# Eight more sorted values before the Newton passes of a sparsemax threshold (audio tower, one core)

## The reference

```
def sparsemax(z):
    n = z.shape[-1]
    z_sorted = jnp.flip(jnp.sort(z, axis=-1), axis=-1)
    cssv = jnp.cumsum(z_sorted, axis=-1)
    r = jnp.arange(1, n + 1, dtype=z.dtype)
    support = 1.0 + r * z_sorted > cssv
    k = jnp.sum(support, axis=-1, keepdims=True)
    tau = (jnp.take_along_axis(cssv, k - 1, axis=-1) - 1.0) / k.astype(z.dtype)
    return jnp.maximum(z - tau, 0.0)
...
sim = jnp.einsum('bhid,bhjd->bhij', q, k) * SCALE
attn = sparsemax(sim)
out = jnp.einsum('bhij,bhjd->bhid', attn, v)
```

## Time and profile before

| | |
|---|---|
| median of 3 runs | 937.27 us (936.76 to 937.72) |
| the profiled execution | 943.18 us, of which the span of its instructions 941.4 us |
| PE busy | 682.3 us (72% of the span) |
| DVE busy | 614.2 us (65%) |
| ACT busy | 456.1 us (48%) |
| POOL busy | 214.3 us (23%) |
| mean granted PE clock | 0.848 |

### The profile page before, as it was taken

The page is one execution under the profiler, slowest core; times in us unless marked ns, Lnnn a source line. Parts: engine busy times, 40 slices in busy tenths (PEclk is TensorE's granted clock), DMA queues, the critical chain, the costliest instruction groups (busy, mean ns, idle before and its releaser), DMA issues.

```text
span 941.4 us, 12887 instructions
## 1 busy us (share of the span) xinstructions
PE 682.3 (72%) x3940; PEld 449.2 (48%) x3940; DVE 614.2 (65%) x2230; ACT 456.1 (48%) x663; POOL 214.3 (23%) x216
## 2 busy tenths in 40 slices
PE   5566959768996988399999998762221897667880
PEld 3234445345564564166575665441110565445660
DVE  2897568777977867697979879855668553423110
ACT  3773648437765756277778677752000331221310
POOL 1111100001000001001010010001003668888876
PEclk9878979978997998799999998885555897788895
DMA  5200000000000000000000000005000133443433
GB/s 153 77 0 1 0 2 1 2 2 13 1 2 12 1 2 12 1 2 13 1 2 13 2 13 2 13 1 151 0 0 20 43 52 67 68 68 65 68 34 28
DMA packets 34858, 23.72 MB, mean 25 GB/s; under 512 B 8246, under 2 KB 31366, under 8 KB 34768
## 3 DMA queue, kind: packets, MB, share of 16 engines
q0 software_dynamic: 11264, 8.40, 6.6%
q1 hardware_dynamic: 23292, 14.28, 5.4%
q10 hardware_dynamic: 212, 0.08, 0.0%
HBM read 14.36 MB, written 8.39 MB: 24 GB/s over the span
## 4 chain that ended last, share of the span: by engine, by line
DVE 30%; PE 29%; issue 12%; ACT 7%; POOL 7%; another core or an unknown queue 5%; DVEq 5%; DMA 2%; ACTq 1%; POOLq 0%; SPq 0%
DVE back L1043 7%; DVE top L1046 5%; PE ps L930 5%; DVE top L1036 4%; POOL out_dram L513 4%; PE ps L740 3%; PE ps L758 3%; PE ps L916 3%; PE ps L785 3%; PE ps L834 2%; PE ps L808 2%; PE ps L818 2%; ACT back L543 2%; DVE front L1236 2%
## 5 line engine op out<-in xcount | busy, mean ns | idle before, releaser
L543 ACT ACTIVATE front<-ps 128x1024 f32<-128x1024 f32 x128 | 127.8, 1026 | 41.0 <-PE ps L785 18.6
L635 ACT ACTIVATE front<-front,minus_tau 128x256 f32<-128x256 f32 x256 | 108.8, 499 | 66.1 <-DVE minus_tau L1125 65.0
L543 ACT ACTIVATE back<-ps 128x1024 f32<-128x1024 f32 x72 | 73.8, 1025 | 90.8 <-issue 74.0
L818 PE MATMUL ps<-ident,front 128*128 128x128 f32 x512 | 77.1, 300 | 52.0 <-ACTq L637 24.2
L513 POOL DMA_INDIRECT out_dram<-back x64 | 103.0, 1609 | 29.7 <-issue 18.3
L449 POOL CROSS_LANE_REDUCE more_all<-more 128x3 int32<-128x3 f32 x32 | 14.7, 460 | 410.7 <-DVEq L1062 410.7
L1043 DVE MATCH_REPLACE8 back<-top,front 128x256 f32<-128x256 f32 x256 | 101.4, 415 | 0.0
L818 PEld LDWEIGHTS ps<-ident,front 128*128 128x128 f32 x512 | 65.3, 155 | 74.8 <-ACTq L637 40.0
L1036 DVE MAX8 top<-front 128x8 f32<-128x256 f32 x256 | 86.8, 413 | 19.7 <-ACT front L543 10.8
L543 ACT ACTIVATE back<-ps,back 128x1024 f32<-128x1024 f32 x32 | 35.4, 1114 | 125.3 <-PE ps L916 57.3
L1046 DVE MAX8 top<-back 128x8 f32<-128x256 f32 x256 | 86.8, 413 | 2.4
(11 more groups left out here) (167 smaller groups left out, 1023.7 us busy)
## 6 DMA issues: line engine op xcount, KB each, us to landing
back<-in_L_ffn_W_dram SPq DMA_DIRECT2D x16, 256.0 KB
front<-in_x_dram SPq DMA_DIRECT2D x4, 750.0 KB, 4.4
rows<-xn SPq DMA_DIRECT2D x8, 256.0 KB, 2.5
out_dram<-h SPq DMA_DIRECT2D x1, 2048.0 KB, 9.6
back<-rows,back POOLq DMA_INDIRECT x64
out_dram<-back POOLq DMA_INDIRECT x64
wqkv<-in_L_attn_W_qkv_dram SPq DMA_DIRECT2D x1, 768.0 KB, 6.0
back<-in_L_ffn_b_dram SPq DMA_DIRECT2D x8, 64.0 KB
```

The lines of the kernel that those rows point to most:

```text
L543: a.activation(dst, ps[s][:, 0:cols], func, **kw).then_inc(sems[f"free{s}"], 1)
L635: a.activation(prob[n % 2][:, r, :], sc[n][:, r, :], ACT.Relu, bias=minus_tau[:, n // 2, n % 2 * 4 + r:n % 2 * 4 + r + 1])
L818: last = nc.tensor.transpose(o[:, a_ * 512 + jb * SEQ + it * P:a_ * 512 + jb * SEQ + (it + 1) * P], prob[n % 2][:, 2 * a_ + it, jb * P:(jb ...
```

## The change

In the refine body DVE no longer goes straight to Newton passes. A new function `third_eight(d)` copies the second eight values and the remaining scores of one half (half 1 if it is noted, otherwise half 0, chosen by a register), replaces the second eight, takes the next eight with `max`, forms the candidates for n = 17 to 24, raises tau where one is larger, and tests whether in any row the 24th value is still above tau. The value go that it leaves is also set where both halves are noted (the product in go_5[4]). Only if go is set do the Newton passes of before follow, for each noted half. The test over all partitions, which each Newton pass ends with, is now a function of its own (`anywhere`), used by both. POOL fills two small constant tiles more at the start.

```diff
+            def anywhere():
+                v.transpose(go_t[:, :], go_w[:, :])
+                v.drain()
+                v.tensor_reduce(r_sum[:, 0:1], go_t[:, :], AX.X, ALU.max)
+                v.drain()
+                for k in range(4):
+                    v.tensor_copy(go_5[0:1, k:k + 1], r_sum[32 * k:32 * k + 1, 0:1])
+                v.drain()
+                v.tensor_reduce(r_sum[0:1, 0:1], go_5[0:1, :], AX.X, ALU.max)
+                v.drain()
+                v.tensor_scalar(go[0:1, :], r_sum[0:1, 0:1], 3e-6, None, ALU.is_gt)
+                v.drain()
+
+            def third_eight(d):
+                u = v.value_load(more_all[0:1, d, 1:2], min_val=0, max_val=1)
+                v.tensor_copy(third[:, :, :], top[:, ds(u * 4, 4), 8:16])
+                v.tensor_copy(sc2[:, 0:4, :], sc2[:, ds(u * 4, 4), :])
+                v.drain()
+                for r in range(4):
+                    v.match_replace(sc2[:, 4 + r, :], third[:, r, :], sc2[:, r, :], LOWEST)
+                v.tensor_tensor(go_5[0:1, 4:5], more_all[0:1, d, 0:1], more_all[0:1, d, 1:2], ALU.mult)
+                v.drain()
+                for r in range(4):
+                    v.max(third[:, r, :], sc2[:, 4 + r, :])
+                v.drain()
+                ta = tau[:, d, ds(u * 4, 4)]
+                sums = cand[:, 0:2, :].rearrange("p r n -> p (r n)")
+                v.tensor_tensor(third[:, :, 0], third[:, :, 0],
+                                csum[:, ds(u * 4, 4), 15:16].rearrange("p r n -> p (r n)"), ALU.add)
+                v.drain()
+                v.tensor_tensor_scan(sums, seg8[:, :, :].rearrange("p r n -> p (r n)"),
+                                     third[:, :, :].rearrange("p r n -> p (r n)"), 0.0, ALU.mult, ALU.add)
+                v.drain()
+                v.scalar_tensor_tensor(sums, sums, -1.0, inv24[:, :, :].rearrange("p r n -> p (r n)"),
+                                       ALU.add, ALU.mult)
+                v.drain()
+                v.tensor_reduce(above[:, 0:4], sums.rearrange("p (r n) -> p r n", n=8), AX.X, ALU.max)
+                v.drain()
+                v.tensor_tensor(ta, ta, above[:, 0:4], ALU.max)
+                v.drain()
+                v.tensor_tensor(above[:, 0:4], third[:, :, 7], ta, ALU.is_gt)
+                v.drain()
+                v.tensor_reduce(go_w[:, 0:1], above[:, 0:4], AX.X, ALU.max)
+                v.drain()
+                anywhere()
...
                 with nc.body(f"refine{n}", valid_engines=[mybir.EngineType.DVE]):
-                    for u in range(2):
-                        with v.If(v.value_load(more_all[0:1, d, u:u + 1], min_val=0, max_val=1) > 0):
-                            again(d, u, 2)
+                    third_eight(d)
+                    with v.If(v.value_load(go[0:1, 0:1], min_val=0, max_val=1) > 0):
+                        v.memset(go_5[0:1, 4:5], 0.0)
+                        v.drain()
+                        for u in range(2):
+                            with v.If(v.value_load(more_all[0:1, d, u:u + 1], min_val=0, max_val=1) > 0):
+                                again(d, u, 2)
                     v.drain()
                     v.br(f"settled{n}")
```

More of the change, by code:

```diff
@@ L264, in audio_tower @@
         inv16 = sb("inv16", [P, 8, 16])
+        inv24 = sb("inv24", [P, 4, 8])
+        seg8 = sb("seg8", [P, 4, 8])
+        third = sb("third", [P, 4, 8])
         r_sum = sb("r_sum", [P, 4])
@@ L268, in audio_tower @@
         go_t = sb("go_t", [P, 32])
-        go_4 = sb("go_4", [P, 4])
+        go_5 = sb("go_5", [P, 5])
         go = sb("go", [P, 1], i32)
@@ L425, in _ @@
             g.memset(seg16[:, :, :], 1.0)
+            g.memset(seg8[:, :, :], 1.0)
             g.iota(iota_r[:, :], [[1, P]], base=0, channel_multiplier=0, allow_small_or_imprecise_dtypes=True)
@@ L434, in _ @@
             g.memset(seg16[:, :, 0:1], 0.0)
+            g.memset(seg8[:, :, 0:1], 0.0)
             for n in range(16):
                 g.memset(inv16[:, :, n:n + 1], 1.0 / (n + 1))
+            for n in range(8):
+                g.memset(inv24[:, :, n:n + 1], 1.0 / (n + 17))
             g.drain()
@@ L1080, in newton @@
                 v.tensor_tensor(r_cnt[:, :], r_sum[:, :], r_cnt[:, :], ALU.mult)
-                v.transpose(go_t[:, :], go_w[:, :])
                 v.drain()
                 v.tensor_tensor(ta, ta, r_cnt[:, :], ALU.add)
[L1085 to L1093, removed]
+                anywhere()
             def again(d, u, depth):
```

## The result

| | before | after |
|---|---|---|
| median | 937.5 us (4 runs) | 948.48 us (4 runs, 947.48 to 949.86) |
| profiled execution, its span | 943.18, 941.4 | 947.48, 945.7 |
| last minus_tau of the 32 steps, its start | 626.1 | 634.7 |
| mean granted PE clock | 0.848 | 0.846 |

The ratio after to before is 1.0106, 95% interval 1.0085 to 1.0127: slower by about 11 us. The forecast was 2.5 us faster, and 948.48 lies above the range. The two profiled executions differ by only 4.3 us, because behind the last minus_tau before's took 315.2 us and after's 310.9, in code that the change does not touch. At the last minus_tau after is 8.6 us late; that is the number which the traces can explain. The other 2.4 us of the medians' difference have no row.

The account below looks back on a forecast made before the run. DVE's own instruction list was taken as the path from 160 to about 400 us, PE from 452; step terms -7.7, -1.8, -1.5, -1.2 and +9.7 give -2.5, so 937.3 becomes 934.8 us, range 931.5 to 945.

Parts of the forecast that it names:

- that the stalls go with the jumps: Refining steps on DVE: jumps over a half's code, 2.84 us at 204.91 and 1.89 at 170.80, disappear with the change.
- a stall inside the new block: Listed among observations that would make the prediction wrong, beside a 1.2 us copy and a late minus_tau at 187.
- By steps: Predicted prices from DVE's previous work to minus_tau: 8.9, 8.9, 10.2, 10.2 and 27.4 us, sum 65.6; before 68.1.
- The block, 7.53 us: DVE's new third_eight work including the test over partitions: 7.53 us, bounds 7.1 to 8.6, against 5.6 for a Newton pass.
- the copy: New block's 128x1024 copy on DVE, one source: 0.67 us, or 1.225 if like the two-source row.
- The step at 396: Both halves noted, so two Newton passes follow the new block: +9.7 us, 27.4 in all, never made up.
- Rival A: Jump out of the new block misses its code, 2.8 instead of 0.40 us at four steps: 944.4, slower; 22%.
- B: Rival: PE cannot follow DVE's earlier tau at 187 and 209, losing 9.5 us there: about +7, 944; 4%.
- D: Rival: go is set in all five steps, by rounding or a leftover in go_5: +47 us, 984; 1%.
- C: New block at its upper bound 8.6 us gives 940.3, at lower 7.1 gives 932.8; spread of the main case.
- The early gains: Steps before 396 get cheaper: -7.7 us at 187, -1.8 at 209, -1.5 at 285, all on the path.
- The steps that don't refine: All others of the 32 steps go straight on, price unchanged: 14.0 us for 25 steps.

Follow-up runs that it names:

- e3: Changed kernel with one copy of the Newton pass per half, repeated by a backward branch, in place of four copies: 939.44 us, ratio to before 1.0009.
- e1: Changed kernel, but a step with both halves noted skips the new block and goes straight to its Newton passes: 949.85 us, ratio to before 1.011.
- e2: Kernel before with one copy of the Newton pass per half, repeated by a backward branch, in place of four: 923.42 us, ratio to before 0.9836.
- e9: e2 with 105 never-run drains behind each half's copy, and the test that skips them: 941.21 us, ratio to before 1.0005.
- e10: e2 with 40 never-run drains behind each half's copy, and the test that skips them: 935.98 us, ratio to before 0.9939.
- e6: Kernel before with six copies of the Newton pass per half in place of four, the added ones never run: 944.63 us, ratio to before 1.0053.

## Why the prediction was wrong

- **The step that failed: that the stalls go with the jumps.** The prediction read 2.84 us at 204.91 and 1.89 at 170.80 as the price of a jump over a half's code, and took them out with the jump ("what goes is not DVE work but the 2.84 us jump"). By the gaps in front of single instructions, sequencer's included, before has five stalls, 1.9, 2.8, 2.6, 2.55 and 3.0: 12.9 us. After has five as well, 1.5, 2.9, 2.6, 2.7 and 2.5: 12.1, of which the prediction kept only 3.0. That is 9.1 of the 10.9 us between 65.6 and 76.5. The prediction named "a stall inside the new block" as what would make it wrong; it gave it no chance and no price. before's trace had what was needed to price it: a stall once in each body, 1.9 at 187 and 2.55 to 3.0 in the others, behind jumps of different length.
- **By steps:** +2.3 at 187 (1.5 at the entry), +5.8 at 209 (2.9 inside, 2.6 at the exit), +0.3 at 285, +2.9 at 351 (2.7 inside), -0.4 at 396, where the stall inside the first pass (2.45) took the place of the jump between the halves, which cost 0.35 this time and not 3.03.
- **The block, 7.53 us:** right (7.6); the copy too (0.69 against 0.67). e3 gives the step prices to within 0.5 us in four steps.
- **The step at 396:** right in part by luck, 27.0 against 27.4: a stall was forecast in one place and another of about its size came. PE stood 24.9 us, as forecast, and nothing was made up.
- **Rival A**, the exit jump that misses (944.4, 22%): it missed in one step of four, by 2.6 us. In the other three the jump over all eight copies found its code in 0.5 to 0.6; whether the hint is why, no run tells. As a whole the rival put 9.6 us on the right cause at the wrong place, and had the sign right. The Trainium skill (Runtime: NRT & Kernel Launch, section Instruction fetch mechanics) says that crossing a block in sequence is mostly hidden and that it is a taken branch out of the two held blocks that stalls. By that rule a jump of 300 stays within two blocks of 256 unless it starts near the end of the first, so the "always misses" of the prediction does not follow from it, and one miss in four is no surprise. By the same rule L1078, L1112 and L1127 should hardly stall; the traces do not agree, with 2.9, 2.8 and 2.4 us in straight code. The packet for each of them starts only after DVE has stopped; whether an earlier branch had left the next block unfetched, no row tells.
- **B and D** did not happen. DVE's prices up to 285 give 5.36 - 4.04 + 1.25 = 2.6 us, after was 0.65 ahead before the first round, and 2.9 us came, so PE followed but for 0.3. go stayed 0 in four steps: the first instruction of a pass stands 8 times, as forecast, and 28 in the earlier trace rows. **C**'s spread was fine for the block.
- **The early gains** were to be 11.0 us by the step behind 285. 2.9 came: minus_tau at 306.4 against 309.3.
- **The steps that don't refine** were taken as unchanged. They cost 1.4 more in after and up to 9.5 more (e1). In e1 three of them have a gap of 2.1 to 2.2 us, each with packets of queue 14 that start less than 1 us before it; for the rest the cause is not shown. I had no term for it.
- **Open:** timed differences to before are larger than those at the last minus_tau in all kernels with a median but e2, by 1 to 5 us (e9: +0.5 timed, -3.0 in the trace). before's one profiled execution may have been a long one in the attention rounds too; no run tells.

## What to carry to other kernels

Where a rarely taken branch is written out once for each use, price its code as well as its work: here about one stall of 2.5 to 3 us for each entry (five in before's five steps, five in four of after's), 5 us for two more copies that never run, and 15 us back for taking three of four away. Make such a body short (a loop with a branch back) before making it clever; that alone gave 1.6% here. An "issue" gap in front of a jump's target is not proof that the jump is what costs, so let it stay in the sum when the jump goes, and ask the DMA view whether an instruction packet starts in it.

## What the runs showed of the hardware

- DVE's sequencer stalls 2.4 to 2.9 us for code in the middle of a straight list, where the last branch was not taken: L1078 2.9, L1112 2.8, L1127 2.4 in after.
- In each of 31 gaps of 2.3 us and more, in straight lists and behind jumps, in the refining steps of the twelve kernels (e2 and e3 have none), an instruction packet of 8,192 bytes starts 0.5 to 1.2 us after DVE stops, and DVE goes on 1.55 to 2.0 us later.
- Dead code costs: 65 drains more in each half of a body, none of which ran, cost 5.2 us of time (e10 to e9); two copies more of a pass, 5 us (e6).
- The jump over half 0 and its 40 dead drains missed at 351 (4.73) and not at 285 (2.41), in one run (e10).
- The jump over some 300 instructions to the drain in front of `settled`, a place that a hint names one settle ahead, found its code in 0.5 to 0.6 us in three of four steps of after; once it took 2.6. No run leaves the hint out.
